# Layer 1 of a four-layer kernel: the experts' output biases, from one transfer per block to one table in SBUF

## The reference, cut to what matters

```
probs = sigmoid(flat @ router_w.T)
scores, idx = top_k(probs, 2)
comb[t, idx] += scores / (sum(scores) + 1e-6)
h  = relu(einsum('td,edh->teh', flat, ew1) + eb1)      # 128 -> 512 in expert e
eo = einsum('teh,eho->teo', h, ew2) + eb2              # 512 -> 128, eb2 is (8, 128)
routed = einsum('teo,te->to', eo, comb)
return shared + routed
```

## Time and profile before

| what | us |
|---|---|
| median of 3 runs | 671.26 |
| lowest and highest of them | 669.85, 674.71 |
| the profiled execution, its time | 674.45 |
| its span, first to last instruction | 672.7 |
| the stretch of the 46 expert blocks in it | about 102 to 262 |

### The profile page before, as it was taken

The page is one execution under the profiler, slowest core; times in us unless marked ns, Lnnn a source line. Parts: engine busy times, 40 slices in busy tenths (PEclk is TensorE's granted clock), DMA queues, the critical chain, the costliest instruction groups (busy, mean ns, idle before and its releaser), DMA issues. The chain is left out here.

```text
span 672.7 us, 12339 instructions
## 1 busy us (share of the span) xinstructions
PE 604.2 (90%) x4045; PEld 381.7 (57%) x4045; DVE 397.0 (59%) x872; ACT 362.3 (54%) x843; POOL 240.6 (36%) x226
## 2 busy tenths in 40 slices
PE   9988978976987999989989888997988998999896
PEld 4654327965857766756756534343666765634343
DVE  2767554823345645856857478645868676456553
ACT  5526736325563453576489344363578479554243
POOL 2000740262265003866647223122148226523121
PEclk9958979987997999999999999999999999999798
DMA  7930313564455510100000300120000000030220
GB/s 254 342 121 0 114 59 110 160 192 147 126 157 156 151 56 28 31 3 2 24 9 1 105 23 1 60 84 0 18 2 1 2 1 1 25 103 1 63 81 16
DMA packets 36927, 47.66 MB, mean 71 GB/s; under 512 B 5089, under 2 KB 23265, under 8 KB 36353
## 3 DMA queue, kind: packets, MB, share of 16 engines
q1 hardware_dynamic: 33888, 39.66, 18.9%
q0 software_dynamic: 2976, 7.21, 3.4%
HBM read 37.55 MB, written 9.31 MB: 70 GB/s over the span
## 5 line engine op out<-in xcount | busy, mean ns | idle before, releaser
L1248 ACT ACTIVATE arena<-bank 128x512 f32<-128x512 f32 (+7 forms) x222 | 123.8, 561 | 97.7 <-PE bank L575 49.4
L575 PE MATMUL bank<-arena,w 128*64 128x128 f32 (+3 forms) x552 | 148.1, 424 | 7.1 <-issue 3.6
L1248 ACT ACTIVATE arena<-bank,arena 128x128 f32<-128x128 f32 (+1 forms) x244 | 87.8, 387 | 119.6 <-PE bank L575 43.7
L575 PE MATMUL bank<-arena 128*64 128x128 f32 (+7 forms) x840 | 97.8, 331 | 5.8 <-ACT arena L1248 5.8
L575 PE MATMUL bank<-xn_b,w 128*128 128x512 f32 (+1 forms) x196 | 95.4, 615 | 5.6 <-DVE arena L2464 5.4
L575 PE MATMUL bank<-arena,work 128*128 128x128 f32 x624 | 85.4, 285 | 13.3 <-DVE arena L2213 10.0
L575 PEld LDWEIGHTS bank<-arena,work 128*128 128x128 f32 x624 | 78.6, 198 | 23.7 <-issue 18.7
L575 PEld LDWEIGHTS bank<-arena,w 128*64 128x64 f32 (+1 forms) x552 | 64.6, 164 | 45.2 <-issue 32.2
L575 PEld LDWEIGHTS bank<-arena 128*64 128x64 f32 (+4 forms) x840 | 58.2, 161 | 37.3 <-ACT arena L1248 23.2
L575 PEld LDWEIGHTS bank<-xn_b,w 128*128 128x128 f32 (+1 forms) x196 | 35.3, 192 | 46.5 <-issue 29.1
L2554 POOL DMA_INDIRECT slots_in<-arena x32 | 32.4, 1012 | 71.6 <-DVE arena L2119 61.8
(11 more groups left out here) (221 smaller groups left out, 854.3 us busy)
## 6 DMA issues: line engine op xcount, KB each, us to landing
work<-in_ew SPq DMA_DIRECT2D x46, 256.0 KB
w<-kept SPq DMA_DIRECT2D x32, 128.0 KB, 3.0
work<-kept SPq DMA_DIRECT2D x32, 128.0 KB, 3.1
slots_in<-work SPq DMA_DIRECT2D x2, 1472.0 KB, 18.4
arena<-in_eb SPq DMA_DIRECT2D x46, 64.0 KB
arena<-slots_in SPq DMA_DIRECT2D x10, 256.0 KB
slots_out<-arena POOLq DMA_DIRECT2D x10, 256.0 KB
w_ew<-in_ew SPq DMA_DIRECT2D x1, 2048.0 KB, 12.5
```

The lines of the kernel that those rows point to most:

```text
L575: return nc.tensor.matmul(o, lhsT, rhs, start=start, stop=stop, skip_group_check=True)
L1248: return nc.scalar.activation(o, i, f, bias=bias, scale=scale, **kw)
```

## The change

The biases of all 8 experts (8 x 128 numbers, 4 KB) are spread over the 128 partitions by one transfer of 512 KB, issued by SP right after the first weights of block 0. SP no longer reads `block_d`, no longer waits for the place in `bias2` and issues no bias transfer per block. DVE reads `block_d` for each block of a group into registers at the head of `evicted(q)`, ahead of the wait for the products, and adds the bias block by block, with the second operand's address from the register. It waits for the one transfer at group 0 alone.

```
-        bias2 = take([3, SB, D])
+        bias2 = take([E1 * D])
...
-        bias2_in = [sem(f"bias2_in_{i}") for i in range(3)]
+        bias2_in = sem("bias2_in")
...
-                    d = nc.values_load(block_d[0:1, n, k % NBLK:k % NBLK + 1], engines=[mybir.EngineType.SP], min_val=0,
-                                       max_val=(E1 - 1) * D)
-                    q, m = group(k), k % NBLK % SB
-                    if m == 0 and q >= 3:
-                        sp.wait_ge(*at_of(0, "rows_out", q - 3))
-                    sp.dma_start(bias2[:, q % 3, m], eb2.rearrange("(a e) d -> a (e d)", a=1)[:, bass.ds(d, D)].to_broadcast([P, D])).then_inc(
-                        bias2_in[q % 3], 16)
+                    if k == 0:
+                        sp.dma_start(bias2, eb2.rearrange("(a e) d -> a (e d)", a=1).to_broadcast([P, E1 * D])).then_inc(
+                            bias2_in, 16)
...
                     def evicted(q):
-                        n = len(blocks_of(q))
+                        if q % NSB == 0:
+                            dve.wait_ge(*at_of(q // NSB, "block_e"))
+                        owners = [nc.values_load(block_d[0:1, k // NBLK, k % NBLK:k % NBLK + 1],
+                                                 engines=[mybir.EngineType.DVE], min_val=0, max_val=(E1 - 1) * D)
+                                  for k in blocks_of(q)]
                         dve.wait_ge(*at("eo", q))
                         if q >= 2:
                             dve.wait_ge(rows_out_sem[q % 2], 16 * (q // 2))
-                        dve.wait_ge(bias2_in[q % 3], 16 * sum(len(blocks_of(i)) for i in range(q % 3, q + 1, 3)))
-                        v.tensor_tensor(rows_out[:, q % 2, 0:n], psum("eo", q)[:, 0:n * P].rearrange(
-                            "p (b d) -> p b d", d=P), bias2[:, q % 3, 0:n], ALU.add).then_inc(*step("rows_out", q))
+                        if q == 0:
+                            dve.wait_ge(bias2_in, 16)
+                        for m, d in enumerate(owners):
+                            v.tensor_tensor(rows_out[:, q % 2, m], psum("eo", q)[:, cs(m)], bias2[:, bass.ds(d, D)],
+                                            ALU.add).then_inc(*step("rows_out", q))
```

## The result

| | changed kernel | kernel before, same comparison |
|---|---|---|
| median, us | 687.89 (4 runs) | 672.61 (4 runs) |
| lowest, highest | 681.45, 692.03 | 669.85, 674.71 |
| ratio, 95% interval | 1.0192, 1.0143 to 1.0241 | |
| profiled execution, its span | 687.96, 686.2 | 674.45, 672.7 |

The changed kernel is slower by 1.9%, and the interval leaves no doubt that it is slower. The forecast was 673.8 us and the range ended at 682.

A forecast was written before the change was run, and what follows sets the result against it. PE, busy 604.2 of 672.7 us, bounds the kernel. Gains -1.5 and -1.5, groups 0 and 1 +2.5, group 2 +0.5, group 4 +0.5, groups 10 and 11 +2.0: +2.5 us, 673.8 us from the median; range 664 to 682.

The forecast's parts named there:

- The price of a read: DVE, head of each eviction: 0.55 us per register read, four in a row 2.2 us, bounds 1.9 and 3.6.
- The adds: DVE evictions: a group's four adds take about 1.15 us in place of 0.68, +0.47, mostly in idle time.
- Groups 0 and 1: Evictions between 119 and 136 us, where DVE is fuller with second-half routing: PE waits, +2.5 us.
- The gains: SP steps without the bias half, group 4's rows earlier: -1.5 us; less traffic in GpSimd's series of indirect transfers: -1.5 us.
- group 2: Eviction at 142.99, directly behind block(13): reads come in full, but PE is refilling, +0.5 us.
- Group 4: Eviction directly behind a block without a pause, so the reads come in full: +0.5 us.
- Groups 5 to 9: Evictions with a DVE wait ahead or over 1 us of slack behind, entered together with group 3: 0.
- (b): Rival: at 0.89 us per read, DVE's reads make PE wait in groups without side work; +11 us, 682; chance 0.22.
- Groups 10 and 11: Last evictions: group 10's reads delay block(45) by 1.7 us, straight on the path; group 11 +0.3; together +2.0 us.
- (a): Rival: less traffic relieves GpSimd's series, shrinking PE's three large holes by a third; 666 us, or 663; chance 0.22.
- (c): Rival: nothing reaches PE, reads run while DVE waits and SP was never the limit; 671 us, within 2; chance 0.13.

The follow-up runs named there:

- e4: Kernel before with each group's add split into its blocks, each from the place of its own bias load: 674.78 us, ratio 0.9989.
- e3: Changed kernel without reads, one add per group from a fixed part of the table, so the choice of the expert's bias is left out: 669.30 us, ratio 0.9957.
- f3: Same kernel as e3, run again in the third set: 667.73 us, ratio 0.9947.
- e1: Changed kernel without its register reads; the four adds take the table's first rows at fixed addresses: 672.04 us, ratio 0.997.
- e2: Kernel before with the 46 register reads added on DVE at the head of the eviction, values unused: 682.80 us, ratio 1.0135.
- e5: Changed kernel with one load of a group's registers in place of its single reads, bounds checks kept: 650.39 us, ratio 0.9993 (kernel before 651.33 us).
- g1: Same code as e5, run in the fourth set: 675.29 us, ratio 1.0049 (kernel before 672.87 us).

## Why the prediction was wrong

**The profile's bottleneck: right.** PE is the bound, and the loss lies in PE's waits.

**The price of a read: nearly right.** Forecast 0.55 us, measured 0.61, so 2.45 per group for 2.2. The load has PE's 300 ns, not the 600 of the Trainium skill's floor ("DMA: Bandwidth & Descriptors", "Latency and other measured facts"); a step of 0.61 us comes about only with the 0.21 of the check and the gaps.

**The adds: dearer in the forecast than on the chip.** Four take 0.88 us in place of 0.68, +0.20 for my +0.47, and e4 finds no time in them.

The rest of the sum can be laid beside the traces. The start of each first(k) in the changed trace less that in the trace before is -0.8 us up to block 7, +3.0 at block 13, +3.15 at 19 to 23, 4.25 at 24 to 29, 3.1 at 30, 6.7 at 31, 7.2 at 32 and 33, 7.8 to 7.95 at 35 to 37, 9.5 at 38 to 40 and 10.8 at 41 to 45.

**Groups 0 and 1: too small.** From block 7 to 13 that is +3.8 us for my 2.5: a wait of 1.70 and 1.4 of half clock behind it, which I had not entered. In group 1, with block(9) at 129.87 and the end of the adds at 133.39, the eviction is 1.5 us later behind its block than before, as forecast (1.4).

**The gains: entered at -3, and nothing of them is left by block 19.** The transposes of group 4 no longer wait, and first(14) stands 1.2 us ahead of the kernel before, 4.2 better than first(13). But the next series of GpSimd takes it back: first(15) and second(13) go in pieces (143.93 with its neighbours), first(16) and first(17) are 2.6 and 4.2 us behind, and from 13 to 19 the sum is +0.15 for my -2.5 (the gains and group 2). The removal by itself is worth its 3 us, as e3 and f3 show (-2.9 and, by its ratio, -3.6). That the reads are what lost it is not shown: in the profile of e1, which has none, first(14) is 1.6 us ahead of the kernel before and first(19) 2.3 behind, after a start 2.8 behind.

**Group 4: +1.1 for my +0.5.** It shows at block 24. PE waits 0.51 us (180.85) for a side instruction of DVE, L2100, that stands behind the eviction.

**Groups 5 to 9, entered at 0: this step failed.** Group 5 did cost nothing (group 3 lies in the series above and can't be told apart). Groups 6 to 9 cost 6.5 us: 3.5 from block 29 to 35, around the evictions of groups 6 and 7 inside GpSimd's gathers, and 3.0 from 35 to 41, at the evictions of groups 8 and 9. They belong to the reads: e2, with reads and all the old transfers, has steps at the same places (+3.3, then +3.0), while e1, without reads, goes from +2.3 at block 29 to +2.6 at 41. How a late eviction becomes 3.5 us inside the gathers I did not take apart. At groups 8 and 9 it can be read.

I had argued that there is a DVE wait ahead of the eviction or over 1 us of slack behind it, and in rival (b) that PE can spare DVE 2.7 us per group, since the bank of block(k+1) is asked for only three blocks on. Both look at DVE's next work or at what the *next block* needs. What PE needs first is the bank of the eviction itself: at 232.72 the first products into the next group's `eo` bank, and at 248.84 the transposes. The trace before had the figure. The eviction of group 9, on DVE and what follows it there, and PE's transposes:

```profile
236.72 0.68 DVE L2224 TENSOR_TENSOR arena<-bank,arena 128x512 f32<-128x512 f32 x1
...
239.16 0.69 DVE L2427 COPY xn_a<-bank 128x512 f32<-128x512 f32 x1 [1.76 <-ACT sq L1248]
```

```profile
238.12 0.49 PE L801 MATMUL bank<-const,arena 128*128 128x128 f32 x3
```

DVE has 1.76 us of idle time behind the eviction, but PE wants the bank 0.72 us after it ends (237.40). The reads push the eviction 1.70 us further from its block and the four adds another 0.20; of these 1.90 us PE waits 1.07, and the rest, 0.8, is about that slack. At group 8 the wait of 1.28 holds a little more: behind the bank PE first reads its own register (TENSOR_LOAD at 232.0), some 0.7 us that it can't hide then. And a DVE wait ahead of an eviction hides reads only if it is long; the earlier trace rows has 0.73 us, against 2.45 of reads.

**Groups 10 and 11: right in kind.** Forecast +2.0 with block(45) 1.7 us later and a wait of PE of 2.5 to 3 us. Measured: 2.70 us of wait for 1.08, second(45) 12.4 us behind where the block's own start was 10.8 behind (+1.6), and +1.1 more to the end, where the products behind the hole run at half clock (32 of them in 3.57 us for 1.96).

So of the 11 us between forecast (+2.5) and measurement (+13.5 in the profiled span), 6.5 are groups 6 to 9, 3.15 the stretch up to block 23 (1.3 of them groups 0 and 1, the rest mostly gains that did not last), 0.6 group 4 and 0.7 the end.

**The rivals.** (b) had the mechanism: reads that stand behind block(k) in DVE's list and pass what PE can spare. It expected a wait after each group without side work; groups 1 and 5 show next to no step, group 0 and groups 6 to 10 do. Its condition, reads of 0.7 us and more, was wrong through the same slack: the loss comes at 0.61. Even by its own 2.7 us the limit was lower, (2.7 - 0.47) / 4 = 0.56 us per read, so the 0.55 of my sum stood at the edge of it and not well below. Its 682 was low. (a) is out by e3 and f3 (ratio 0.9957 and 0.9947, where it wanted 0.98 to 0.99), (c) by the result.

## What to carry to other kernels

A register read on an engine with an ordered list is a hold that no busy time shows: count its whole step, check included, times the reads in a row, and compare that with the time until another engine needs *any* result behind it, the bank just being emptied first of all. Take that time from the other engine's rows, not from the idle time of the engine that reads. Spread the reads over the list, one ahead of each wait, or load several registers at once; here either took the loss away or most of it. A transfer that runs hidden beside other work is worth little: removing 45 of them here paid 3 us, less than what the reads that replaced them cost.

## What I had not expected of the hardware

- **The same kernel differs between sets of runs.** The kernel before took 671 to 674 us in the comparison of the result and in three of the four sets, and 651.33 in one. Whether that was another chip or another condition of the same one these runs don't tell. The windows of one program, e5 and g1 (same code), from 140 to 160, first in the 651 us set, then in the 673 us set:

```profile
140.00:160.00 20.00, 19.64 (x125) 14.41 (x124) 9.06 (x24) 12.96 (x28) 9.73 (x10) 1.00 0.46 145
```

```profile
140.00:160.00 20.00, 14.99 (x77) 12.01 (x77) 6.51 (x21) 9.17 (x21) 10.62 (x12) 0.83 0.53 163
```

  GpSimd issues its indirect transfers at the same pace on both (1.27 us apart), but only on the second do PE and DVE stall beside them, and only there does the granted clock fall, to a mean of 0.83. So the late signals that the prediction found in the series are no property of the program alone. What makes them late stays open.
- **A load of four registers takes 0.34 us at some places and 1.0 at others**, in the same order in three programs and three sets; one of three takes 0.75, one of one 0.30. The slow ones are all in the first half's row of the table, the fast ones all in the second's. What decides it stays open.
- **A short wait of PE can bring half clock behind it.** At group 0 the changed kernel has it behind a wait of 1.70 us in all three of its profiles (8 products in 2.04 to 2.07 us), and loses 3.1 us there in the first; e2 waits 1.38 and 0.53 at the same place and keeps full clock.
- **The bounds check costs 0.21 us per value on DVE** (190 + 23 ns), two thirds of the load itself.
